# A graph network's second dense stage: statistics, normalisation and bf16 parts of h moved from behind the stage into it, and shared by two engines

## The reference

```
h = relu(layernorm(x));  x = x + segment_sum(edge_weight * h[src], dst)            # first dense stage
h = relu(layernorm(x));  x = x + edge_mlp_layer(h, ...)                             # per edge
h = relu(layernorm(x));  x = x + relu(segment_sum(w * (h @ W)[src], dst) + bias)    # second dense stage
h = relu(layernorm(x))
for l in range(3):                                                                  # count stage, three layers
    out = h + segment_sum(h[src] + edge_attr, dst)
    z = gelu(layernorm(out @ W1[l].T + b1[l]))
    z = layernorm(z @ W2[l].T + b2[l])
    h = gelu(z + h)
x = x + h
```

## Time and profile before

| | us |
|---|---|
| median of 3 runs | 5626.27 (5624.34 to 5633.94) |
| the profiled execution | 5629.7, its span 5627.9 |
| TensorE busy | 4909.3 (87% of the span) |
| VectorE busy | 3168.0 (56%) |
| ScalarE busy | 1754.6 (31%) |
| GpSimd busy | 2089.6 (37%) |

### The profile page before, as it was taken

One profiled execution on the slowest core, in us unless ns is written; L12 is line 12 of the kernel. 1 busy time (PEld: TensorE's weight loads), 2 busy tenths in 40 slices (PEclk: granted clock), 3 DMA queues, 4 the chain that ended last, 5 costly groups with the idle time before them and its releaser, 6 DMA issues.

```text
span 5627.9 us, 139608 instructions
## 1 busy us (share of the span) xinstructions
PE 4909.3 (87%) x42810; PEld 4173.0 (74%) x42810; DVE 3168.0 (56%) x9378; ACT 1754.6 (31%) x3785; POOL 2089.6 (37%) x2575
## 2 busy tenths in 40 slices
PE   1899999998888888888888888659998999999998
PEld 1799999998777777777777777459996666666665
DVE  7899999996555555555555555630003444444444
ACT  2555555555111111111111111210001444445445
POOL 6211111111777777777777777000000111111000
PEclk8999999999999999999999999879998999999999
DMA  6344444444555555555555555037775554554554
GB/s 169 148 205 198 193 191 205 205 199 166 132 132 132 132 133 133 131 133 132 133 132 132 133 131 133 12 137 294 291 292 188 189 183 176 189 183 178 188 183 160
DMA packets 464598, 943.57 MB, mean 168 GB/s; under 512 B 107346, under 2 KB 395970, under 8 KB 426898
## 3 DMA queue, kind: packets, MB, share of 16 engines
q1 hardware_dynamic: 187778, 696.55, 32.9%
q0 software_dynamic: 58304, 121.69, 9.0%
q10 hardware_dynamic: 218448, 124.48, 8.2%
HBM read 691.90 MB, written 250.56 MB: 167 GB/s over the span
## 4 chain that ended last, share of the span: by engine, by line
PE 65%; issue 10%; POOL 9%; DVE 5%; DMA 4%; ACT 3%; DVEq 3%; ACTq 1%; POOLq 0%; SPq 0%
PE ps L1142 20%; PE ps L975 10%; PE ps L997 10%; POOL BIG L695 9%; PE ps L960 7%; PE ps L1075 4%; DMA BIG<-table,IDX 4%; PE ps L1073 4%; PE ps L1085 4%; PE ps L958 2%; DVEq L378 2%; PE ps L1074 1%; ACT ACC L805 1%; PE ps L1029 1%; DVE BIG L1482 1%
## 5 line engine op out<-in xcount | busy, mean ns | idle before, releaser
L695 POOL DMA_INDIRECT BIG<-table,IDX x1664 | 1615.9, 971 | 535.5 <-issue 470.3
L1491 DVE TENSOR_TENSOR ACC<-ACC,ps 128x257 f32 x1664 | 702.4, 422 | 588.9 <-PE ps L1085 571.1
L1073 PE MATMUL ps<-T,BIG 128*128 x3328 | 698.7, 293 | 342.0 <-DMA BIG<-table,IDX 194.5
L1073 PEld LDWEIGHTS ps<-T,BIG 128*128 128x128 f32 x3328 | 539.8, 200 | 458.0 <-issue 449.7
L1085 PE MATMUL ps<-BIG 128*128 128x257 f32 x3328 | 808.3, 385 | 0.0
L1075 PE MATMUL ps<-BIG,ident 128*128 128x128 f32 x3328 | 771.4, 315 | 0.0
L975 PE MATMUL ps<-H,ACC 128*128 128x128 f32 x4802 | 690.5, 284 | 0.0
L1085 PEld LDWEIGHTS ps<-BIG 128*128 128x128 f32 x3328 | 615.3, 195 | 73.6
L833 ACT ACTIVATE IDX<-SRC 128x4 int32 (+1 forms) x416 | 85.1, 205 | 1827.9 <-PE ps L1075 1144.3
L960 PE MATMUL ps<-T,BIG 128*128 128x98 bf16 x9408 | 633.0, 206 | 0.0
L958 PE MATMUL ps<-BIG 128*128 128x98 bf16 x3136 | 569.4, 207 | 70.1 <-ACT ACC L805 53.2
(11 more groups left out here) (233 smaller groups left out, 6318.9 us busy)
## 6 DMA issues: line engine op xcount, KB each, us to landing
weight_mat<-ACC SPq DMA_DIRECT2D x49, 3136.0 KB, 9.3
BIG<-weight_mat SPq DMA_DIRECT2D x49, 3136.0 KB, 10.2
BIG<-count_mat SPq DMA_DIRECT2D x73, 1568.0 KB, 6.5
REL_WT<-count_mat SPq DMA_DIRECT2D x72, 1568.0 KB, 6.6
count_mat<-BIG SPq DMA_DIRECT2D x49, 1568.0 KB, 12.8
BIG<-rel_tab ACTq DMA_DIRECT2D x416, 128.0 KB, 3.1
BIG<-in_edge_attr SPq DMA_DIRECT2D x832, 64.0 KB
BIG<-in_edge_attr ACTq DMA_DIRECT2D x832, 64.0 KB
```

The lines of the kernel that those rows point to most:

```text
L695: pool.indirect_dma_start(G[:, q * QUAD + u, :], None, tables[1], bass.IndirectOffsetOnAxis(ap=IDX[:, q, u:u + 1], axis=0)).then_inc(gathe ...
L1073: pe.matmul(to, DT[:, q % 2, u * P:(u + 1) * P], T1[:, b[q * QUAD + u], :], start=True, stop=False)
L1491: dve.tensor_tensor(to, to, PS[4 + u][:, 0:2 * F + 1], ALU.add).then_inc(slots_free, 1)
```

## The change

Four things are done.

1. Each block is normalised as its sum comes. Behind bn_stats of a block VectorE runs bn_aggr, reciprocal and nmr on one column, with ScalarE's root between them, and ScalarE then writes the block's H. The 49-wide steps remain in the general way alone. Two column slots (b % 2) hold the statistics.
2. The parts are split by two engines: ScalarE makes the two bf16 copies (high_parts), VectorE the two subtractions (rest_parts). Both take chunk c + 1's first operation ahead of chunk c's second.
3. The parts of the first EARLY = 8 chunks are made between block 47 and block 48, in the code of both engines; the other five behind block 48. Eight chunks are 6144 columns and fit in the first half of BIG (6272). For this the halves of BIG are swapped between the two WIN, so that block 47 uses the first half and block 48 the second. ScalarE's first part waits for wsum_ps of block 47.
4. CIN[0] and CIN[1] are swapped, and the second load of counts waits for block 48's products, since its place, the last quarter of BIG, lies in the half that block 48 uses. TensorE waits for VectorE to have emptied block 48's bank before it starts on output block 0.

```diff
-        WIN = [BIG[:, k * NP:(k + 1) * NP] for k in range(2)]
+        WIN = [BIG[:, (1 - k) * NP:(2 - k) * NP] for k in range(2)]
-        CIN = [BIG[:, 3 * NP // 2:2 * NP].bitcast(BF16), REL_WT[:, 0:NP // 2].bitcast(BF16), ACCf[:, 3 * NP // 2:2 * NP].bitcast(BF16)]
+        CIN = [REL_WT[:, 0:NP // 2].bitcast(BF16), BIG[:, 3 * NP // 2:2 * NP].bitcast(BF16), ACCf[:, 3 * NP // 2:2 * NP].bitcast(BF16)]
+        EARLY = NP // (CHUNK * 3 * F // 2)
...
                 sp.wait_ge(wsum_ps, 2 * BLOCKS + 1)
                 load(0, 0, 0)
+                sp.wait_ge(wsum_ps, 2 * BLOCKS + 2)
                 load(0, 1, 1)
...
-            stds(5)
-            relu_norm(5)
+            def normed_block(b, par, i):
+                wait_alone(act, aggr_done, 24 + (b + 1))
+                act.activation(rstd[:, par:par + 1], MV[:, par, 1:2], ACT.Sqrt, bias=epsc[:, 0:1]).then_inc(std_ready, 1)
+                wait_alone(act, norm_ready, 4 + (b + 1))
+                act.activation(H[:, b, :], X[:, b, :], ACT.Relu, bias=nmr[:, par:par + 1], scale=rstd[:, par:par + 1]).then_inc(h_ready, 1)
+            def high_parts(chunks_):
+                def part(k, c):
+                    nb = CHUNK if c < CHUNKS else 1
+                    of = ACC[:, c * CHUNK:c * CHUNK + nb, 0:F] if k else blk(H, c, nb)
+                    if k:
+                        act.wait_ge(part2, c + 1)
+                    else:
+                        act.wait_ge(h_ready, 3 * C1 + c * CHUNK + nb)
+                    act.activation(HP[0][:, c * CHUNK:c * CHUNK + nb, k, :], of, ACT.Copy).then_inc(part3 if k else part1, 1)
+                for c in chunks_:
+                    part(0, c)
+                    if c > chunks_[0]:
+                        part(1, c - 1)
+                part(1, chunks_[-1])
+            def normed_blocks():
+                with act.Fori(0, BLOCKS // 2) as i:
+                    normed_block(i * 2, 0, i)
+                    normed_block(i * 2 + 1, 1, i)
+                act.wait_ge(wsum_ps, 2 * BLOCKS + 1)
+                high_parts(range(EARLY))
+                normed_block(BLOCKS - 1, 0, BLOCKS // 2)
+                act.wait_ge(wsum_ps, 2 * BLOCKS + 2)
+                high_parts(range(EARLY, C1))
...
                 pe.wait_ge(cblk_in[0], 16)
+                pe.wait_ge(wsum_used, 2 * BLOCKS + 2)
...
-            def first_parts(c, nb, par):
+            def rest_parts(chunks_):
+                def part(k, c):
+                    nb = CHUNK if c < CHUNKS else 1
+                    own = slice(c * CHUNK, c * CHUNK + nb)
+                    rest = ACC[:, own, 0:F]
+                    if k == 0:
+                        dve.wait_ge(part1, c + 1)
+                        dve.tensor_tensor(rest, blk(H, c, nb), HP[0][:, own, 0, :], ALU.subtract).then_inc(part2, 1)
+                    else:
+                        dve.wait_ge(part3, c + 1)
+                        dve.tensor_tensor(HP[0][:, own, 2, :], rest, HP[0][:, own, 1, :], ALU.subtract).then_inc(parts_ready, 1)
...
-                    dve.bn_stats(ST[:, b, :], X[:, b, :]).then_inc(stats_done, 1)
-                block_pairs(dve, body)
+                    dve.bn_stats(ST[:, par, :], X[:, b, :]).then_inc(stats_done, 1)
+                    wait_alone(dve, stats_done, 4 * BLOCKS + (b + 1))
+                    dve.bn_aggr(MV[:, par, :], ST[:, par, :]).then_inc(aggr_done, 1)
+                    wait_alone(dve, std_ready, 4 + (b + 1))
+                    own = slice(par, par + 1)
+                    dve.reciprocal(rstd[:, own], rstd[:, own]).then_inc(part_done, 1)
+                    wait_alone(dve, part_done, 4 + (b + 1))
+                    dve.scalar_tensor_tensor(nmr[:, own], MV[:, par, 0:1], -1.0, rstd[:, own], ALU.mult, ALU.mult).then_inc(norm_ready, 1)
+                with dve.Fori(0, BLOCKS // 2) as i:
+                    body(i * 2, 0, i)
+                    body(i * 2 + 1, 1, i)
+                rest_parts(range(EARLY))
+                body(BLOCKS - 1, 0, BLOCKS // 2)
+                rest_parts(range(EARLY, C1))
...
-            statistics(X, 5, True)
-            rstds(5)
...
-                chunks(dve, first_parts)
```

More of the change, by code:

```diff
@@ L880, in _, with normed_all @@
             copy_out(hT_ps, hT_sb, HT, 0, base=2 * C1)
-            stds(5)
-            relu_norm(5)
+            def normed_block(b, par, i):
[26 more added lines that the diff above has]
+                high_parts(range(EARLY, C1))
+            def normed_all():
+                stds(5)
+                relu_norm(5)
+            two_ways(act, overfull, normed_blocks, normed_all)
             act.wait_ge(layer_in, LAYERS * 128)
@@ L1610, in summed_steps @@
                 per_block(lambda b: dve.bn_stats(ST[:, b, :], X[:, b, :]).then_inc(stats_done, 1))
+                statistics(X, 5, True)
+                rstds(5)
             two_ways(dve, overfull, summed_blocks, summed_steps)
-            statistics(X, 5, True)
-            rstds(5)
             def stages(l, out_sum):
```

## The result

The changed kernel takes 5599.56 us (median of 5, 5598.38 to 5602.27), the one before 5626.27: 26.7 us less, a ratio of 0.9953 with a 95% interval of 0.9942 to 0.9964. A second series gave 5599.58 against 5627.19. The forecast was 5600, range 5596 to 5608. In the experiments two single executions, 11267 us of the kernel before and 12374 us of woven_count, ran in a slow state at a low clock; the medians count them, the ratios leave them out.

The account below looks back on a forecast made before the run. TensorE was taken to wait 41.0 us between weight and count stages, on VectorE's serial tail and 13 chunks. Gains of 25.4 + 0.6 = 26.0 us off the 5626.3 median gave 5600.3, forecast 5600, range 5596 to 5608.

Parts of the forecast that it names:

- Normalising in the weight stage: Blocks 0 to 47: 1.4 us more VectorE work per block, hidden by the block's products, costing nothing on the path.
- The sign I had named: Weight stage: the prediction would be wrong if a weight block got longer than 11.1 us.
- Start of the early parts: Behind block 47: its nmr ready at 4274.0, the ReLU issued by 4274.4, and the first bf16 copy then starts.
- E: End of the eight early chunks: 4285.8 without GpSimd, plus 1.6 for about six subtractions beside its copies, so 4287.4.
- Block 48 and the last five chunks: Behind the early chunks: block 48's sum, statistics and ReLU, then five chunks, ending 10.2 us later at 4297.6.
- second block: Count stage: TensorE starts its second block at 4297.7 instead of 4323.1, 25.4 us less.
- Clock bonus: Second count block: less time at TensorE's low clock, a gain of 0 to 1.66 us, 0.6 taken.
- Loads: First two count blocks: landing 6.6 us after issue, at 4283 and 4289, 5 and nine us early; cost 0.
- GpSimd's lock: Rival: GpSimd's copies hold every VectorE operation from 4282.1 to their end by 0.5, giving 5604 us; 14%.
- the clock was low: Rival: TensorE's clock stays low until the second count block, ending 6.5 us later, giving 5607 us; 11%.
- the slower case: Rival: engine hand-overs set the chunk pace, 3.9 us a chunk and 5631 us (1%), mildly 2.2 and 5609 (7%).
- the tables: Rival: roots and ReLUs need different tables, two loads of 1.28 us every block, giving 5605 us; 3%.

Follow-up runs that it names:

- woven_count: woven with the first count block loaded ahead of the layer weights: 5598.7 us, against 5626.1 for the kernel before.
- norm_only: Changed kernel with only per-block normalising; VectorE alone makes all thirteen chunks' parts, behind block 48: 6231.6 us, against 6234.3 for the kernel before.
- pool_late: Changed kernel with GpSimd's thirteen copies to T1 put behind the last part: 5600.7 us, against 5627.2 for the kernel before.
- both: Changed kernel with GpSimd's copies behind the parts and the first count block loaded ahead of the layer weights: 5598.2 us, against 5627.2 for the kernel before.
- early6: Changed kernel with six chunks ahead of block 48 instead of eight: 6208.0 us, against 6234.3 for the kernel before.
- one_engine: Changed kernel with VectorE making all four operations of a chunk, eight chunks ahead of block 48: 6213.7 us, against 6234.3 for the kernel before.
- split_late: Changed kernel with no chunk ahead of block 48 (EARLY = 0): 6214.6 us, against 6234.3 for the kernel before.
- woven: Changed kernel with block 48's steps put one by one between the chunks on both engines: 5598.1 us, against 5626.1 for the kernel before.
- woven_all: woven_count with GpSimd's copies behind the last part: 5593.0 us, against 5626.1 for the kernel before.
- woven_pool: woven with GpSimd's copies behind the last part, count block loaded in the changed kernel's order: 6171.0 us, against 6200.9 for the kernel before.

## Why the prediction was right, point by point

- *Normalising in the weight stage costs nothing*: confirmed as far as the scatter lets one tell: the median block takes 10.94 us with and without it, and the stages 538.4 and 539.6 us. The sign I had named, a block over 11.1 us, is no use: the longest takes 11.2 in both. Block 47 took 1.37 us from the end of its statistics to the end of nmr (4269.20 to 4270.57), 1.4 predicted; the hand-over from root to reciprocal was 0.15 us and the mean idle of VectorE around the root 0.57, in sum as I took it. The tail's part of the gain is 4.5 us (norm_only).
- *Start of the early parts*: first copy 3.2 us behind the start of block 47's sum (4267.97 to 4271.19), predicted 3.2 (4271.24 to 4274.4); no table load in the weight stage or the early parts.
- *E, the end of the early parts*: predicted 5.4 us behind the last weight product, measured 3.4. Two terms were too large. I took 3.8 without GpSimd, since I put the pitch between 0.60 and 0.69; it is 0.60, and the runs pool_late and both, without the lock, end the early parts at 3.0 and 3.2. And I took 1.6 for GpSimd, for six subtractions; only the last one was held, by 0.2 us (0.92 instead of 0.69). Here it was GpSimd that waited.
- *Block 48 and the last five chunks*: predicted 10.2 us from E, measured 11.0 (3.4 to 14.4). Here the lock was left out and should not have been: it holds nmr and about five subtractions, and the last part comes 2.1 us sooner without it in the run both, 2.3 in pool_late. So the lock costs somewhat more than the 1.6 taken, and nearly all of it in the place where I took nothing.
- *TensorE*: second block predicted at 15.7, measured 15.9 and 15.0. It started 2.2 us sooner than I said and was not the bound; early6 shows that its start does not matter in this order. That 15.7 came out is luck in part. The last part was predicted at 15.6 and came at 14.4, since E was 2.0 us too late and the last chunks 0.8 too short. Against that I put only 0.1 us between the last part and the second block; the products that are left then took 1.6 in the first profile, at the low clock, and 0.7 in the second. The errors cancelled.
- *Clock bonus*: 1.66 us in full (8.13 instead of 9.79), 0.6 taken, the largest part of what the sum lacks against C4; but 0.9 us goes to the low clock at the last products of the first block, in one profile and not in the other, and that stands in A.
- *Loads*: wrong in size, right in effect by little. I took the median of 6.6 us from issue to landing, but this load took 9.4 already in the kernel before; in the changed kernel it took 9.5 and 7.6. It landed not 5 us ahead of its use but 0.2 and 2.0, and in pool_late it was what TensorE waited for.
- *Sum*: 26.0 predicted; measured 26.7 and 27.6 in the two series, 27.1 and 28.1 on C4. A small slip is in it: 4323.1 is the edge of a window, the second block started at 4323.45, so the forecast should have been 0.35 us more. By parts: the tail 4.5, the split 16.7, the early start 5.9 to 6.8, in this order of adding them; in the other order the early start is worth 14.9 and the split 7.8 (one_engine).

The rivals: GpSimd's lock is real, and it holds the late subtractions and nmr, for 2.1 to 2.3 us in all and not the 5 of the rival; the clock was low for 10 or 11 of the 49 products in the changed kernel's two profiles, not for a whole block; the hand-overs between the engines cost nothing at a pitch of 1.20 us a chunk (split_late), so the slower case was far off; the tables did not switch.

## What to carry to other kernels

When elementwise work stands between two TensorE stages, there are two ways to shorten it, a second engine and an earlier start. Here either alone was worth about 15 us (16.7 and 14.9) and the other on top of it 6 to 8, so what a part is worth depends on which one is there already. Put per-tile work into the stage that produces the tile, but look what stands behind it in its engine's queue. An idle gap on an engine may be what lets another engine's copies through: before filling it, see who uses the gap, and move both together. When a bound is taken away and little is gained, look for the next one before calling the first harmless: without the lock it was TensorE's start and its clock.

## What the runs showed of the hardware

- GpSimd's fp32 copies of 128x512 and VectorE's subtractions with two SBUF inputs exclude each other: 0.68 us becomes 1.09, and the thirteen copies need 7.0 us alone, 11.5 in the changed kernel, 12.2 in woven. VectorE's operation on columns of one element beside a copy (nmr) goes from 0.16 to 0.51. The sum with a PSUM input and bn_stats keep 0.27 to 0.29 us. The Trainium skill, "SBUF — State Buffer", section "Who interferes with whom", says that a VectorE instruction with two SBUF inputs contends with a GpSimd instruction that reads SBUF, and the trace agrees. VectorE's fp32 copies to bf16 take part as well: beside GpSimd's copies they take 0.83 instead of 0.41 us in one_engine, and GpSimd's thirteen need 16.05.
- Who gives way changed within one run. In one_engine VectorE kept its 0.41 and 0.68 us for 6.5 us while GpSimd's first copy waited; behind block 48's sum the same operations took 0.83 and 1.09 us, and the copies beside them 0.8 to 1.07. In woven both sides were held from the second copy on. What decides between the two was not settled.
- TensorE's clock stayed at its full level through a pause of 3.7 us in one profile and was low (0.50) for the first ten products behind it in the next, with the same instructions. In woven_all and woven_pool, with pauses of 0.94 and 2.32 us, it stayed full through both count blocks. What makes it fall was not settled.
